# Three-token attention: transposes of the sums and their copy stand first in the slots of TensorE and ScalarE

## The reference, cut to what matters

```
for kk in range(4):                       # scales 1, 3, 9, 27
    scale = 3 ** kk
    pQ, pK, pV = mean of Q, K, V over groups of `scale` tokens
    o = mha over windows of 3 tokens, 6 heads:
        qp, kp, vp = q @ wq.T + bq, k @ wk.T + bk, v @ wv.T + bv
        attn = softmax(qp . kp / sqrt(32))      # 3 x 3 per head
        o = (attn . vp) @ mow.T + mob
    acc = acc + gelu(o spread back over the tokens)
out = acc @ ow.T + ob
x + out
```

## Time and profile before

| | |
|---|---|
| median of 3 runs | 1155.31 us (1151.77 to 1155.31) |
| profiled execution | 1158.98 us, span 1157.1 us |
| mean granted clock of TensorE | 0.927 |
| PE busy | 998.3 us (86%) |
| DVE busy | 636.4 us (55%) |
| POOL busy | 565.4 us (49%) |
| ACT busy | 466.9 us (40%) |
| this part (first projection to the end of `accT`) | 341 to 477 us |

### The profile page before, as it was taken

The page is one execution under the profiler, slowest core; times in us unless marked ns, Lnnn a source line. Parts: engine busy times, 40 slices in busy tenths (PEclk is TensorE's granted clock), DMA queues, the critical chain, the costliest instruction groups (busy, mean ns, idle before and its releaser), DMA issues.

```text
span 1157.1 us, 24046 instructions
## 1 busy us (share of the span) xinstructions
PE 998.3 (86%) x6992; PEld 854.6 (74%) x6993; DVE 636.4 (55%) x1649; ACT 466.9 (40%) x1172; POOL 565.4 (49%) x1094
## 2 busy tenths in 40 slices
PE   7899999999997987599888888888349999999960
PEld 4789889889975654488677776766339999999950
DVE  7477585575437787466667666665412222222216
ACT  1234323233213444345565555555114444444424
POOL 2578586676421223414666666666504444434330
PEclk9989999999988998799899999998569999999985
DMA  8564662470103300306200000000011111111118
GB/s 356 205 266 189 225 275 95 190 306 34 39 11 62 63 1 0 58 1 266 105 13 16 16 16 16 16 16 19 26 48 38 41 43 43 36 43 42 44 35 253
DMA packets 41701, 103.09 MB, mean 89 GB/s; under 512 B 7046, under 2 KB 28656, under 8 KB 38837
## 3 DMA queue, kind: packets, MB, share of 16 engines
q1 hardware_dynamic: 30085, 88.86, 22.1%
q0 software_dynamic: 5760, 9.68, 2.5%
q10 hardware_dynamic: 5808, 3.96, 1.1%
HBM read 86.30 MB, written 18.32 MB: 90 GB/s over the span
## 4 chain that ended last, share of the span: by engine, by line
PE 35%; POOLq 22%; issue 21%; POOL 7%; DVE 6%; DMA 4%; ACT 2%; DVEq 1%; SPq 1%; ACTq 0%
PE pe L1631 16%; POOLq L561 6%; POOLq L537 4%; PE pe L1640 4%; POOLq L526 2%; DMA x<-yy_d 2%; POOL xn L532 1%; POOLq L539 1%; POOLq L510 1%; POOLq L551 1%; POOL xs_d L529 1%; DVE sc L316 1%; PE pe L183 1%; DMA raw<-in_xw 1%; PE pe L184 1%
## 5 line engine op out<-in xcount | busy, mean ns | idle before, releaser
L1631 PE MATMUL pe<-wm,xm 128*128 128x193 f32 x1008 | 174.1, 331 | 1.7 <-issue 1.7
L1631 PEld LDWEIGHTS pe<-wm,xm 128*128 128x128 f32 x1008 | 168.0, 192 | 6.4 <-issue 6.4
L844 ACT ACTIVATE hT<-pe,eb 128x128 f32<-128x128 f32 x336 | 92.8, 375 | 147.6 <-PE pe L970 147.5
L983 PE MATMUL pp<-w2s,hT 128*128 x672 | 118.5, 326 | 0.0
L983 PEld LDWEIGHTS pp<-w2s,hT 128*128 128x128 f32 x672 | 107.9, 190 | 0.2
L967 PE MATMUL pe<-xsT,ew 128*128 128x128 f32 x672 | 89.4, 284 | 3.3 <-ACT xsT L834 3.3
L967 PEld LDWEIGHTS pe<-xsT,ew 128*128 128x128 f32 x672 | 81.1, 195 | 8.6 <-ACT xsT L834 4.1
L759 DVE TENSOR_TENSOR ys<-pp,b2s 128x192 f32<-128x192 f32 x56 | 20.0, 358 | 121.4 <-PE pp L983 118.5
L529 POOL DMA_INDIRECT xs_d<-xsrc,dst x64 | 65.6, 1025 | 41.7 <-issue 41.7
L557 POOL DMA_INDIRECT yy_d<-ys,yix x56 | 57.2, 1022 | 46.5 <-issue 46.5
L1355 POOL TENSOR_TENSOR sqs<-sqs,sqt 128x448 f32<-128x448 f32 x56 | 67.5, 1205 | 8.0
(11 more groups left out here) (267 smaller groups left out, 2220.3 us busy)
## 6 DMA issues: line engine op xcount, KB each, us to landing
xm<-in_xm SPq DMA_DIRECT2D x7, 2688.0 KB, 14.0
raw<-in_xwa SPq DMA_DIRECT2D x7, 1792.0 KB, 7.2
raw<-in_xwb SPq DMA_DIRECT2D x7, 1536.0 KB, 11.4
x<-in_x SPq DMA_DIRECT2D x4, 1536.0 KB, 8.6
xs<-xs_d SPq DMA_DIRECT2D x56, 96.5 KB
x<-yy_d SPq DMA_DIRECT2D x8, 672.0 KB
w1s<-in_W SPq DMA_DIRECT2D x1, 4608.0 KB
w2s<-in_W SPq DMA_DIRECT2D x1, 4608.0 KB
```

Source lines behind the costliest of these rows:

```text
L844: last = f(self.hT[:, u, c], pe1[:, 2 * u + c % 2, (c // 2) * ROWS:(c // 2 + 1) * ROWS], ACT.Gelu, bias=self.b1[:, u, c:c + 1])
L983: last = mm(pp[:, u, 0:D], self.hT[:, u, n], self.w2s[:, bass.ds(e, 1), n * D:(n + 1) * D].rearrange("p o d -> p (o d)"), start=(n == 0), ...
L1631: mm(y[:, 0:D + 1], cell(q, c), wm[:, q, c], start=(q + c == 0), stop=(q == 3 and c == KC - 1))
```

## The change

Two moves in code that every slot runs. On TensorE the transposes of item t-3 now come before the qkv groups 0 and 1 of item t. On ScalarE the copy `oT` of item t-3 comes before the copies of groups 0 and 1, the exp and the staging. Nothing else changes: the same instructions, the same waits, the same buffers. In the slots without an item t or t-3 the order on TensorE stays as it was. The transposes have line 197 in the new text (202 before), the copy `oT` line 252 (266 before), and the exp line 259 (257 before).

```diff
--- before.py
+++ after.py
@@ -188,11 +188,6 @@
 
         def slot(item):
             a, c = item(0), item(3)
-            if a:
-                i, u, _ = a
-                pe.wait_ge(self.stg_set, i + 1)
-                qkv(i, u, 0)
-                qkv(i, u, 1)
             if c:
                 i = c[0]
                 pe.wait_ge(self.w_o, i + 1)
@@ -201,6 +196,11 @@
                     for s in range(3):
                         last = nc.tensor.transpose(pt1[:, h, s * P:(s + 1) * P], self.ob[:, s, h * LOW:h * LOW + P], ident)
                 last.then_inc(self.o_T, 1)
+            if a:
+                i, u, _ = a
+                pe.wait_ge(self.stg_set, i + 1)
+                qkv(i, u, 0)
+                qkv(i, u, 1)
             if a:
                 qkv(*a[:2], 2)
             if c:
@@ -247,9 +247,11 @@
 
         def slot(item):
             a, b, c = item(0), item(1), item(3)
+            if c:
+                act.wait_ge(self.o_T, c[0] + 1)
+                nc.scalar.activation(self.oT[:], pt1[:, :, 0:3 * P], ACT.Copy).then_inc(self.o_out, 1)
             if a:
                 qkv(*a[:2], 0)
-            if a:
                 qkv(*a[:2], 1)
             if b:
                 i, u, _ = b
@@ -262,8 +264,6 @@
                 self.stage(act, i + 1, 1 - u)
             if c:
                 i, u, _ = c
-                act.wait_ge(self.o_T, i + 1)
-                nc.scalar.activation(self.oT[:], pt1[:, :, 0:3 * P], ACT.Copy).then_inc(self.o_out, 1)
                 if i >= NWT - 3:
                     gelu(i - (NWT - 3))
             if a:
```

## The result

The changed kernel takes 1141.31 us (median of 4 runs, 1140.69 to 1144.56), the kernel before 1153.54 us beside it (4 runs, 1151.43 to 1155.31): a ratio of 0.990 with a 95% interval of 0.9871 to 0.993, or 12.2 us less. The same text run twice more gave 0.991 [0.9894, 0.9926] and 0.9905 [0.9886, 0.9925], so nearer 11 than 12. Forecast were 7.5 us less and 1147.8 us; the time is under the low end of 1143.5.

A forecast was written before the change was run, and what follows sets the result against it. Bound: the attention's chain of waits. Savings of 5.7 to the last exp, 0.7 and 1.5 at the end make 7.9, or 7.0 at half clock; 7.5 taken: 1158.98 to 1151.5 profiled, 1147.8 by the median; range 1143.5 to 1153.5.

The forecast's parts named there:

- The chain of waits: Three-token attention, 340 to 477 us: one unbroken chain, so each microsecond taken from it is one of the kernel.
- L212(9) at half clock: End of the stretch: item 9's output projection takes 4.37 instead of 2.3 after idle; saving then 7.0, otherwise 7.9.
- The period: Repeating part of the attention: 9.28 us an item instead of 9.93, bounded below by 8.73.
- TensorE's floor: TensorE's slot in the repeating part: 9.28 us from projections to next projections, including 0.26 idle behind the drain.
- Prod to prod 9.3 in every item: Sign of success in the repeating part: 9.3 us between prods, instead of 9.38 and 10.47 in turns.
- The end: Last exp to accT: 0.7 and 1.5 saved beyond the exp's 5.7, in all 7.9; accT starts at 458.1.
- accT's wait for the third GELU: Closing sums: the ninth op of accT waits 0.9 us if item 9's output projection runs at half clock.
- Head of the queue: Rival, chance 0.05: a late sum blocks transposes first in TensorE's slot; 2 us waiting a slot gives 1164.8.
- DVE and POOL do collide: Rival, chance 0.10: small DVE ops slowed by POOL's adds, about 9.9 an item; saving only 2.5, 1152.8.
- Given back behind the stretch: Rival, chance 0.05: the gain is lost behind 477 us through weights, clock or a broken chain; 1155.
- I let the rest of the kernel shift as a whole: Everything behind 477 us: shifts unchanged with the mixing matmuls; weight loads could take back at most 1.5.
- the base: Whole kernel: starting time for the forecast, the runs' median 1155.31, 3.67 under the profiled 1158.98.

The follow-up runs named there:

- e1: Kernel before with only TensorE's edit: transposes first, the copy oT left behind exp and staging; ratio 0.9946 to the kernel before.
- e2: Kernel before with only ScalarE's edit: the copy oT first, transposes left behind qkv groups 0 and 1; ratio 1.0038 to the kernel before.
- e8: Changed kernel without TensorE's drain behind the third qkv group, staging waiting for that projection's own semaphore; ratio 0.9917 to the kernel before.
- e10: Changed kernel without the drain, ScalarE's gall copies of item 8 moved before the exp and first two GELUs together; ratio 0.9888 to the kernel before.
- e5: Changed kernel with POOL's first add done three times, same result; one run, 1171.37 us.
- e3: The kernel before, unchanged, profiled and timed again; ratio 0.9994 to the kernel before.
- e4: The changed kernel, unchanged, profiled and timed again; ratio 0.991 to the kernel before.
- e12: The changed kernel, unchanged, profiled a third time; ratio 0.9905 to the kernel before.
- the delays: Changed kernel with the last accT sum repeated 1, 2, 4, 6 or 8 more times; ratios 0.9934, 0.9952, 0.9932, 0.9954, 0.997 to the kernel before.

## Why the prediction missed the time

**The chain of waits was the right bound.** 7.5 off the stretch was forecast; from first projection to first mixing matmul 7.7, 7.5 and 7.5 are measured in three profiles. e1 and e2 show that it comes from the waits named: with the transposes alone 4.5, with the copy alone a loss. That the sizes agree so well is in part luck: 7.5 was the middle of two cases, and the one that came true, L212(9) at half clock, was priced 7.0.

**The period.** TensorE's floor was put at 9.28 and is 9.23. DVE's waiting was put at 0.5 an item over its own 8.73 and is that: its bracket of 0.81 holds the 0.32 which an item without any queue has as well. "Prod to prod 9.3 in every item" holds from the fifth step on only, as the first items go at 8.7 to 9.1. The last exp was forecast 5.7 earlier and is 6.2 earlier, counted from the first projection (114.22 to 108.04). The floor was read from the slot in the earlier trace rows, drain and all, and e8 shows that 0.5 of it is the drain.

**The end.** accT starts 116.3 behind the first projection; 116.7 was forecast. L212(9) at half clock came true and so did accT's wait for the third GELU, 0.46 instead of 0.9. What the end's account left out is the contention of g: beside POOL's add it takes 4.37 instead of 2.23, and ends just behind the second GELU (455.90 against 455.76), so it cost 0.1 and was close to costing more.
In TensorE: Matmul & The Clock Gate, Part 4: PE-mode transpose, the Trainium skill has transposes not counting as busy for the clock; the trace agrees in so far as L212(9) ran at 2.85 behind the lone T(9), but the 4.64 of idle between them would explain it as well, and no run here parts the two. In e10 the same transposes have only 1.52 of idle time ahead of them and 0.95 behind, and the matmuls behind took 2.53, which fits the page without deciding it.

**The rivals.** Head of the queue did not occur with both edits; e2 shows it on ScalarE, where I had not looked for it. My margin against it, 4.5 us until the transposes, was counted to the wrong deadline: the sum's first is pv, 1.8 us on, so a sum 3.1 us longer already costs what I had priced for one 5.7 us late (e5). DVE and POOL do collide in every item (L320 0.69 where it takes 0.22 alone), inside the 9.23. Given back behind the stretch: the opposite.

**The step that failed** is "I let the rest of the kernel shift as a whole", with the base that I added it to. It is the term for everything behind 477 us, sized 0; the low end of the range had room for the drain and the runs' spread, and none for it. The runs show 1.7 there, in the first stage behind. The forecast lies 6.5 over the measured 1141.3:
- 1.8 is the base. I took the 1155.31 of three runs; beside the changed kernel it was 1153.54.
- 1.7 is mixing (51.4 to 49.7). It is the other level of the clock in L898 (3.21 to 1.96, 1.25) and in L907 right behind it (1.28 to 0.82). It is not a matter of the moment: e3 repeats the 3.2, e4 and e12 the 1.96.
- 0.2 is the part.
- That leaves 2.8 of this comparison. Over the three comparisons of the changed kernel the ratios of 0.990, 0.991 and 0.9905 make 11.5, 10.4 and 11.0 us, 11.0 in the mean, and 11.0 less 7.7 less 1.7 is 1.6. The 9.4 of part and mixing lie within all three intervals, and beside e3's profile nothing is left over, so it is not shown that these 1.6 us are there at all. It may be other groups which meet the clock at another moment; the delays, with rests from -4.3 to +0.6, and e8 with +2.5, leave that open. Whether something is left, and what, stays open, and so does why the clock stood otherwise in L898.

## What to carry to other kernels

In a software pipeline with in-order engines, read which instruction a wait really blocks: an operation that was ready stood behind eight matmuls that waited for something else. Move producer and consumer together, or the gain turns into a loss (e2). And where TensorE's clock switches, a shift by a few microseconds can be worth one or two microseconds in stages that nobody touched. So before you explain a rest of under 0.3% of a kernel, repeat the unchanged kernel: here its own two profiles differed by 7.4 us outside the part.

## What the runs showed of the hardware beyond that

- The drain behind matmuls that frees a buffer costs 0.5 us an item (TensorE's slot 9.23 to 8.76), while its idle bracket shows 0.26. Without it the output projection's first weight load starts 0.24 ahead of its matmul (395.10 and 395.34 in e8), with it 0.03 (431.40 and 431.43 in after).
- With two-input adds on DVE and POOL at the same time, both slow down: two sums g take 4.37 beside POOL's add, and 2.23 in the kernel before, where none lies beside them; that add takes 2.14, where POOL's others take 1.40.
- Matmuls put in only to keep the clock up did so for the group right behind them (0.56 for 0.98) and not for the next but one (3.09 and 3.31 for 1.96).
- One text is 3.3 to 4.8 us slower on one chip than on the three others (medians of 1158.06 against 1154.75, 1154.41 and 1153.24).
